# Gate scores as one stacked matmul: query and keys split in halves from the fourth tile on

## What is computed

```python
q = jnp.einsum('bsd,rd->bsr', x, Wq_w)
scores = jnp.einsum('bsr,er->bse', q, keys)
top_vals, top_idx = jax.lax.top_k(scores, TOP_K)
top_w = jax.nn.softmax(top_vals, axis=-1)
...
z = jnp.einsum('bsd,nd->bsn', x, A_w)
...
out = jnp.einsum('bsn,on->bso', z_gated, B_w) * SCALING
```

## Time and profile before

| | |
|---|---|
| median of 3 runs | 241.18 us (241.16 to 241.32) |
| the profiled execution | 241.43 us |
| its span in the trace | 239.4 us |
| mean granted TensorE clock | 0.999 |
| PE busy | 234.9 us, 98% of the span |
| DVE busy | 177.2 us, 74% |
| ACT busy | 98.1 us, 41% |
| DMA | 160 GB/s mean |
| PE, share of the chain that ended last | 91% |

### The profile page before, as it was taken

One profiled execution on the slowest core, in us unless ns is written; L12 is line 12 of the kernel. 1 busy time (PEld: TensorE's weight loads), 2 busy tenths in 40 slices (PEclk: granted clock), 3 DMA queues, 4 the chain that ended last, 5 costly groups with the idle time before them and its releaser, 6 DMA issues.

```text
span 239.4 us, 4288 instructions
## 1 busy us (share of the span) xinstructions
PE 234.9 (98%) x1558; PEld 216.7 (91%) x1558; DVE 177.2 (74%) x403; ACT 98.1 (41%) x241; POOL 1.6 (1%) x9
## 2 busy tenths in 40 slices
PE   8999999999999999999999999999999999999995
PEld 7999999698998989899898989989898998989885
DVE  1589699999959697895959699595959959352522
ACT  4598957253544162624415352432535241202000
POOL 2000000000000000000000000000000000000000
PEclk9999999999999999999999999999999999999999
DMA  6998016274733717245371815446182342616222
GB/s 224 373 411 337 2 47 221 72 260 162 215 130 99 252 59 241 100 133 178 103 251 59 261 76 151 159 108 246 62 253 84 93 169 47 219 44 219 92 88 88
DMA packets 22628, 38.24 MB, mean 160 GB/s; under 512 B 2512, under 2 KB 10576, under 8 KB 22608
## 3 DMA queue, kind: packets, MB, share of 16 engines
q1 hardware_dynamic: 22464, 37.89, 47.7%
q10 hardware_dynamic: 144, 0.08, 0.2%
HBM read 25.64 MB, written 12.32 MB: 159 GB/s over the span
## 4 chain that ended last, share of the span: by engine, by line
PE 91%; DVE 3%; DMA 2%; issue 2%; SPq 1%; POOL 0%; ACT 0%; DVEq 0%; POOLq 0%
PE p_z L581 33%; PE p_out L621 12%; PE p_out L620 12%; PE p_out L628 11%; PE p_conv L531 10%; PE p_conv L484 4%; PE p_out L581 2%; DMA a_raw<-z_dram 2%; PE p_t L637 2%; PE p_out L484 1%; PE p_z L604 1%; PE p_t L640 1%; PE p_t L593 1%; DMA z_dram<-a_raw 1%; SPq L266 1%
## 5 line engine op out<-in xcount | busy, mean ns | idle before, releaser
L620 PE MATMUL p_out<-b_hi,zt_hi 128*128 128x512 f32 (+1 forms) x128 | 50.2, 393 | 0.0
L621 PE MATMUL p_out<-b_hi,zt_lo 128*128 128x512 f32 (+1 forms) x128 | 50.1, 392 | 0.0
L581 PE MATMUL p_z<-a_hi,h_lo 128*128 128x264 f32 x240 | 35.8, 290 | 0.0
L581 PE MATMUL p_z<-a_hi,h_hi 128*128 128x264 f32 x240 | 34.1, 285 | 0.5 <-DVE z_g L805 0.5
L628 PE MATMUL p_out<-b_lo,zt_hi 128*128 128x512 f32 (+1 forms) x128 | 34.4, 391 | 0.0
L581 PE MATMUL p_z<-a_lo,h_hi 128*128 128x264 f32 x240 | 33.9, 284 | 0.0
L581 PEld LDWEIGHTS p_z<-a_hi,h_hi 128*128 128x128 f32 x240 | 31.9, 188 | 1.9 <-issue 0.9
L581 PEld LDWEIGHTS p_z<-a_hi,h_lo 128*128 128x128 f32 x240 | 32.1, 189 | 0.0
L581 PEld LDWEIGHTS p_z<-a_lo,h_hi 128*128 128x128 f32 x240 | 31.1, 188 | 0.0
L694 DVE TENSOR_TENSOR x_lo<-x_blk,x_hi 128x1536 fp32r<-128x1536 f32 (+2 forms) x18 | 25.6, 1421 | 5.5 <-ACT x_hi L323 5.4
L323 ACT ACTIVATE h_hi<-h_t 128x1024 fp32r<-128x1024 f32 x16 | 17.0, 1060 | 30.6 <-DVE h_t L735 30.6
(11 more groups left out here) (94 smaller groups left out, 318.0 us busy)
## 6 DMA issues: line engine op xcount, KB each, us to landing
x_nat<-in_x_rows SPq DMA_DIRECT2D x16, 512.0 KB, 5.2
out_dram<-x_nat SPq DMA_DIRECT2D x31, 256.0 KB, 3.1
x_blk<-in_x_blocks SPq DMA_DIRECT2D x14, 516.0 KB, 3.9
z_dram<-a_raw SPq DMA_DIRECT2D x60, 64.0 KB, 1.8
a_raw<-z_dram SPq DMA_DIRECT2D x15, 256.0 KB, 3.5
a_raw<-in_a_wq SPq DMA_DIRECT2D x8, 264.0 KB, 6.6
x_nat<-in_b_w SPq DMA_DIRECT2D x4, 512.0 KB, 9.9
x_blk<-in_x_blocks SPq DMA_DIRECT2D x4, 258.0 KB, 4.3
```

Source lines behind the costliest of these rows:

```text
L581: mm = nc.tensor.matmul(z_bank(t, b)[:, 0:HB], h[:, t % 2, r, :], a[:, r, b * HB:(b + 1) * HB], start=k == 0 and r == 0, stop=k == 2 and r ...
L620: nc.tensor.matmul(dst, zt_hi[:, t % 2, c, :], b_hi[:, c, cols], start=c == 0, stop=False)
L621: nc.tensor.matmul(dst, zt_lo[:, t % 2, c, :], b_hi[:, c, cols], start=False, stop=False)
```

## The change

Three kinds of edit are made; tiles 0 to 2 keep the plain fp32 scores, and all later tiles (TS = 3) take the new way.

One: the query is written into q_s as high part, low part, high part, in columns 0 to 15, 16 to 31 and 32 to 47. ACT writes the high part twice in one instruction with a broadcast source, and DVE writes the low part (`split_q`). After the turn these are rows of q_t. The keys are stacked to match, once: high, high, low, in k_r (`split_keys` on both engines). One fp32r matmul over these rows sums the three products.

Two: `turn_q` stands after all 16 matmuls of the second group on bank 0, where it stood in the middle of them, and waits for DVE as well (s_qlo).

Three: `take_q(3)` on ACT is moved ahead of `split_h(4)` and `split_z(1)`, which stood before it; on DVE `split_q(3)` stands ahead of the same two, and in the loop `split_q(i + 1)` stands between `split_x(i + 3)` and `split_h(i + 2)`.

```diff
+TS = 3
...
-        q_s = sb("q_s", [P, P])
-        q_t = sb("q_t", [P, P])
+
+        q_s = sb("q_s", [P, P], F32R)
+        q_f = sb("q_f", [P, P])
+        q_t = sb("q_t", [P, P], F32R)
+        k_r = sb("k_r", [P, E], F32R)
...
-                nc.scalar.activation(q_s[:, 0:RD], z_bank(i, 1)[:, J - HB:HB], ACT.Copy).then_inc(s_q, 1)
+                query = z_bank(i, 1)[:, J - HB:HB]
+                if i < TS:
+                    high(q_s[:, 0:RD].bitcast(F32), query, s_q)
+                else:
+                    high(q_s[:, 0:4 * RD].rearrange("p (k d) -> p k d", d=2 * RD)[:, :, 0:RD],
+                         query.unsqueeze(1).to_broadcast([P, 2, RD]), s_q)
...
             def copy_q(i):
                 act.wait_ge(s_qtp, i + 1)
-                nc.scalar.activation(q_t[:], p_t[:, 0:P], ACT.Copy).then_inc(s_qt, 1)
+                high(q_f[:] if i < TS else q_t[:], p_t[:, 0:P], s_qt)
+
+            def split_keys():
+                act.wait_ge(s_small, 16)
+                high(k_r[:], sm[:, SMALL_K:SMALL_K + E], s_khi)
...
             split_x(1, 1)
+            split_keys()
             add_u(0, 0)
...
             split_x(5)
+            take_q(3)
             split_h(4)
             split_z(1)
             for i in range(3, NT):
-                take_q(i)
+                if i > 3:
+                    take_q(i)
...
             def turn_q(i):
                 pe.wait_ge(s_q, i + 1)
+                if i >= TS:
+                    pe.wait_ge(s_qlo, i - TS + 1)
...
-                nc.tensor.matmul(scores_at(i), q_t[:], sm[:, SMALL_K:SMALL_K + E], start=True, stop=True).then_inc(s_scp, 1)
+                if i == TS:
+                    pe.wait_ge(s_klo, 1)
+                queries, keys = (q_t[:], k_r[:]) if i >= TS else (q_f[:], sm[:, SMALL_K:SMALL_K + E])
+                nc.tensor.matmul(scores_at(i), queries, keys, start=True, stop=True).then_inc(s_scp, 1)
...
-                z_product(i, 1, (0,), range(R // 2))
+                z_product(i, 1, (0,), range(R))
                 turn_q(i)
-                z_product(i, 1, (0,), range(R // 2, R))
                 z_product(i, 2, (0,), range(R))
...
+            def split_keys():
+                dve.wait_ge(s_khi, 1)
+                low(k_r[2 * RD:3 * RD], sm[2 * RD:3 * RD, SMALL_K:SMALL_K + E], k_r[2 * RD:3 * RD], s_klo)
+
+            def split_q(i):
+                dve.wait_ge(s_q, i + 1)
+                low(q_s[:, RD:2 * RD], z_bank(i, 1)[:, J - HB:HB], q_s[:, 0:RD], s_qlo)
```

More of the change, by code:

```diff
@@ L158, in adaln_ffn @@
         s_q = sem("s_q")
+        s_qlo = sem("s_qlo")
+        s_khi = sem("s_khi")
+        s_klo = sem("s_klo")
         s_qz = sem("s_qz")
@@ L311, in _ @@
             nc.gpsimd.memset(ident[:], 0.0).then_inc(s_iz, 1)
-            nc.gpsimd.memset(q_s[:], 0.0).then_inc(s_qz, 1)
+            nc.gpsimd.memset(q_s[:].bitcast(F32), 0.0).then_inc(s_qz, 1)
             pool.wait_ge(s_iz, 1)
@@ L592, in turn_q @@
                     pe.wait_ge(s_qt, i)
-                nc.tensor.transpose(p_t[:, 0:P], q_s[:], ident[:]).then_inc(s_qtp, 1)
+                nc.tensor.transpose(p_t[:, 0:P], q_s[:].bitcast(F32), ident[:]).then_inc(s_qtp, 1)
             def turn_last():
@@ L894, in _ @@
             split_x(5)
+            split_q(3)
             split_h(4)
@@ L935, in _ @@
                     sum_w(1)
+                if i + 1 < NT:
+                    split_q(i + 1)
                 if i + 2 < NT:
@@ L979, in laid_out @@
     small[:, SMALL_B:SMALL_B + 2 * NG] = np.tile(bias.reshape(2 * NG, CI).T, (R, 1))
-    small[0:RD, SMALL_K:SMALL_K + E] = keys.T
+    for k in range(3):
+        small[k * RD:(k + 1) * RD, SMALL_K:SMALL_K + E] = keys.T
     return {"x_blocks": x_blocks, "x_rows": x_rows, "conv_w": w, "a_wq": a, "b_w": b, "small": small}
```

## The result

In the paired runs the changed kernel took 237.69 us in the median of 6 (237.36 to 239.43), the kernel before 241.17 in the median of 6 (239.35 to 241.32). The ratio is 0.9895, with a 95% interval from 0.9852 to 0.9939.

What follows compares the result with a forecast made beforehand. TensorE, busy 98% of the span, was taken to bound the kernel. Scores 1.37 plus tile 3 0.55 gave 1.92 us saved, so 241.18 - 1.92 = 239.26 us, range 238.8 to 239.9 (chance 0.80).

Steps and rivals of the forecast that it cites:

- The scores: Scores matmuls from tile 3 on: one fp32r pair costs 0.11 to 0.12 us, saving 0.105 in 13 tiles, 1.37 us.
- The turn and its cover: Query transpose four matmuls later, eight left before the scores: costs nothing, operands 1.2 us early, copy 0.3 us to spare.
- The keys: One-time key split, a copy on ACT and a subtraction on DVE, 0.2 to 0.3 us each, hidden in idle time.
- Tile 3: First tile of the loop: TensorE's wait for the query before the turn goes, 0.55 us saved, bounds 0 and 0.62.
- The sum: Whole kernel: 1.37 + 0.55 = 1.92 us saved, 241.43 to 239.5 for its own execution, 239.26 from the median.
- the sign: Whole kernel: faster by over 0.2% (0.5 us), chance 0.93; slower, chance 0.04.
- the rivals: Four: tile 3 keeps its wait (0.12), narrow pair cheaper (0.08), scores no cheaper (0.05), scores wait for ACT's copy (0.04).
- the 0.03 for what was not seen: Whole kernel: chance 0.03 kept for outcomes outside forecast and rivals, split over both sides.
- The rival with a cheaper narrow pair: Scores: a narrow pair costs 0.06 us, less than a load, saving 2.1 us, 238.5 with tile 3; chance 0.08.

Runs made afterwards that it cites:

- the doubled pair: Changed kernel with 16 warm-up matmuls, each stacked scores matmul issued twice from tile 3 on: 240.17 us, against 238.99 without the doubling.
- the late turn: Changed kernel with 16 warm-up matmuls, turn four matmuls later, so four instead of eight first-product matmuls stand before the scores: 241.22 us, against 238.99.
- e1: The kernel before, run again unchanged, with a trace: 240.75 us in the median of 12, traced span 238.4 us.

## Why the prediction was off

**The scores** (1.37): right. 1.41 behind tile 3, 0.11 a tile; the doubled pair cost 0.11.

**The turn and its cover** (nothing): right, with margins of 1.3 and 0.4 us, where 1.2 and 0.3 were counted, and the late turn shows what the second is worth.

**The keys** (nothing, under cover): right, 39.26 against 39.28 us for the stretch that holds them.

**Tile 3** (0.55): right for that trace, 0.57, but too small as a size for the kernel. The bounds read "0 (DVE late by half a microsecond) and 0.62 (the whole difference)". The old wait is a DMA's landing, and tile 3 took 6.58 to 7.89 in six traces, mean 7.1, against 6.02 with the query taken first. The gain grows with the landing until the new order waits too. A landing of 5.24 gives 7.63 by the line and took 6.09 and 0.16 behind it, so 1.4 us is gained there, and I estimate no more for a later one. By that the order is worth 0.6 to 1.4 us, 1.0 on average of the six landings. I saw the DMA in the earlier trace rows and still took its one duration for a constant.

**The sum** ("Against its own execution: 241.43 - 1.92"): this is the step that failed and that put the median outside the range. It carries everything ahead of tile 3 over unchanged, but that part is 2.1 to 2.3 us longer or shorter by the instant at which the slow pace ends. The trace of before was one with a late rise, as its slow pace until 10.4 shows. Of the paired runs of the changed kernel four of six lie in the group of early starts, 237.4 to 237.9, and five of six of the kernel before above 241; of these twelve runs only one was traced, the changed kernel's at 237.36. Like with like, the paired runs give about 1.8 (241.2 and 239.4) and 1.9 (239.35 and 237.4) us, close to the forecast. Three runs within 0.16 us had made me take the kernel for steady. The range held bounds for the terms and none for the execution.

**The chances**: the sign was right, and none of the rivals came about. What happened lies in the 0.03 for what was not seen. The rival with a cheaper narrow pair would have given the measured time more nearly, for a reason that is refuted. That 1.92 lies so near the 1.9 between the means is in part luck, as its term for tile 3 came from a trace with the shortest landing of six.

Open: what decides between an early and a late start, why the landing differs from run to run, and what the two runs of the changed kernel above 241 us were, as no trace caught one. By the traces about 2.4 us between like starts would follow (1.41 + 1.0), by the groups of runs 1.8 to 2.1, by the means of all runs 1.87 +- 0.5, with 16 warm-up matmuls 2.8 and 2.3; these agree only roughly.

## What to carry to other kernels

A matmul of 64 columns cost its weight load here, 0.11 us, so small products are best joined by stacking them along rows of the contraction that lie empty, which saves loads. Where a short operation that TensorE waits for stands in an in-order list behind one that waits for a DMA, put it first: here it took most of the transfer's spread out of the path, not only the wait seen in one trace. Before forecasting to half a percent, cut the span at a few marks and ask of each piece whether another execution would give it again; the start at the low clock and the DMA on the path are where it didn't here.

## What the runs showed of the hardware

The time at which TensorE left the slow pace differed between executions of one program (before and e1), from 3.9 to 10.4 us after the first instruction, and moved the end by 2 us. Twice the warm-up cut the standard deviation of the changed kernel from 1.5 us (1.1 without its two runs above 241) to 0.4 (12 runs each), at a median of 238.7 and 239.0 against 237.9 over all its plain runs. A 256 KB transfer issued at the same place of the program, at tile 3's first matmul, landed between 4.2 and 5.5 us later. Plain fp32 operands took two weight loads and two matmuls for one call, 0.22 us at 64 columns, fp32r operands one of each, 0.11 us.
